# Last layer of a four-layer attention kernel: output product ahead of the pieces, back transposes at the end of a round, pieces and row statistics placed anew

## What is computed

```
ln_out = layernorm(hidden_states, ln1_s, ln1_b)
qkv = ln_out @ w_qkv + b_qkv
ctx = merge_heads(attention(q, k, v, ltor_mask))          # 16 heads of 16
x = hidden_states + ctx @ w_ao + b_ao
q = layernorm(x, ln2_s, ln2_b) @ w_q + b_q;  k, v = split(encoder_states @ w_kv + b_kv)
x = x + merge_heads(attention(q, k, v, cross_mask)) @ w_co + b_co
return x + gelu(layernorm(x, ln3_s, ln3_b) @ w1 + b1) @ w2 + b2
# attention: scores / 4, scores * mask - 10000 * (1 - mask), softmax, @ v
```

## Time and profile before

| | us |
|---|---|
| median of 3 runs | 1341.6 (1341.17 to 1344.08) |
| the profiled execution, its own time | 1344.38 |
| its span in the profile | 1342.6 |
| PE busy | 1249.9 (93% of the span) |
| DVE, ACT, POOL busy | 837.7, 738.5, 568.8 |
| rounds of the last layer | from 1057.58 (first piece of FIRST) to 1342.6 |

### The profile page before, as it was taken

How to read it: one execution, slowest core, us unless ns; L and a number is a source line. 1 busy time by engine, 2 the same in 40 slices (tenths; PEclk the granted TensorE clock), 3 DMA queues, 4 the chain that set the end, 5 groups by cost and what they waited for, 6 DMA issues and landing times.

```text
span 1342.6 us, 24499 instructions
## 1 busy us (share of the span) xinstructions
PE 1249.9 (93%) x8912; PEld 1021.4 (76%) x8912; DVE 837.7 (62%) x1864; ACT 738.5 (55%) x2000; POOL 568.8 (42%) x583
## 2 busy tenths in 40 slices
PE   6999999999887988999999999999998978988788
PEld 5777777777644557899999889999996646767667
DVE  4666666766549976666666776666675137687521
ACT  4665666566546875545454655455544244666621
POOL 3664555555359963232120413131203146677501
PEclk9999999999998999999999999999999989998999
DMA  6101010100010004111111111120001001000000
GB/s 261 50 27 52 27 52 27 53 27 29 3 65 0 1 1 157 33 48 33 48 32 49 33 48 43 37 72 9 17 1 65 0 0 64 2 1 1 1 12 20
DMA packets 15525, 50.44 MB, mean 38 GB/s; under 512 B 1840, under 2 KB 5296, under 8 KB 14384
## 3 DMA queue, kind: packets, MB, share of 16 engines
q1 hardware_dynamic: 15408, 48.87, 11.0%
HBM read 47.82 MB, written 1.05 MB: 36 GB/s over the span
## 4 chain that ended last, share of the span: by engine, by line
PE 81%; DVE 11%; ACT 4%; issue 2%; POOL 1%; DMA 1%; SPq 0%; DVEq 0%; ACTq 0%
PE pS L1534 13%; PE pT L1562 6%; PE acc L1614 6%; PE acc L326 6%; PE pC L406 4%; PE pT L393 4%; PE pS L376 4%; PE pS L1576 4%; PE pC L1599 4%; PE heads_scores L1355 3%; PE acc L362 3%; PE heads_scores L1344 3%; PE pT L1587 2%; PE heads_scores L2041 2%; DVE stats L1248 2%
## 5 line engine op out<-in xcount | busy, mean ns | idle before, releaser
L1534 PE MATMUL pS<-split_sources,split_pair_weights 128*128 128x512 f32 x768 | 212.0, 411 | 5.8 <-issue 4.3
L722 POOL TENSOR_TENSOR probs<-probs,stats 128x512 f32<-128x512 f32 x128 | 130.5, 1040 | 140.1 <-DVE stats L587 140.1
L528 ACT ACTIVATE probs<-pS,stats 128x256 f32<-128x256 f32 x256 | 117.8, 472 | 102.0 <-DVE stats L582 102.0
L1534 PEld LDWEIGHTS pS<-split_sources,split_pair_weights 128*128 128x128 f32 x768 | 135.9, 190 | 30.7 <-issue 6.6
L1711 ACT ACTIVATE probsT<-pT 128x256 f32<-128x256 f32 x128 | 49.1, 384 | 197.2 <-PE pT L1587 197.2
L1614 PE MATMUL acc<-l_wo_parts,l_ctx_parts 128*128 128x256 f32 x768 | 122.0, 295 | 1.0 <-DVE l_ctx_parts L1783 1.0
L1562 PEld LDWEIGHTS pT<-l_wv_parts,split_sources 128*128 128x128 f32 x756 | 106.9, 188 | 14.2 <-issue 2.2
L1562 PE MATMUL pT<-l_wv_parts,split_sources 128*128 128x256 f32 x756 | 110.6, 281 | 2.1 <-issue 2.1
L1837 POOL TENSOR_TENSOR split_pair_weights<-weights_a,split_pair_weights 128x1024 fp32r<-128x1024 f32 x16 | 38.0, 2378 | 170.1 <-ACT split_pair_weights L1675 170.0
L1614 PEld LDWEIGHTS acc<-l_wo_parts,l_ctx_parts 128*128 128x128 f32 x768 | 99.4, 190 | 1.2 <-DVE l_ctx_parts L1783 1.2
L326 PE MATMUL acc<-split_sources,split_pair_weights 128*128 128x512 f32 x372 | 99.5, 402 | 0.8 <-POOL split_pair_weights L704 0.7
(11 more groups left out here) (253 smaller groups left out, 2899.1 us busy)
## 6 DMA issues: line engine op xcount, KB each, us to landing
weights_a<-in_l_w SPq DMA_DIRECT2D x16, 768.5 KB, 4.3
weights_a<-in_l_w SPq DMA_DIRECT2D x16, 768.0 KB, 5.9
value_bias_rows<-in_l_bv SPq DMA_DIRECT2D x16, 256.0 KB, 4.4
weights_b<-in_l_wo SPq DMA_DIRECT2D x16, 256.0 KB, 2.7
w_fc<-in_l_w SPq DMA_DIRECT2D x4, 1024.0 KB, 5.9
bias_rows<-in_rows SPq DMA_DIRECT2D x1, 1536.0 KB, 13.3
x_residual<-in_x_dbl SPq DMA_DIRECT2D x2, 512.0 KB, 7.0
masked_scores<-in_ctx_dbl SPq DMA_DIRECT2D x2, 512.0 KB, 7.9
```

The source lines that it names most:

```text
L528: a = e.activation(self.E[:, n % 4, h, it, :], self.S[h][:, it, :], ACT.Exp, bias=self.st[:, 1, n % 4, h, it:it + 1], accum_out=self.st[:, ...
L722: e.tensor_tensor(self.E[:, n % 4, h, :, :], self.E[:, n % 4, h, :, :], self.st[:, 3, n % 4, h, :].unsqueeze(2).broadcast_to([P, 2, D]), A ...
L1534: mm = e.matmul(bank[:, :], self.w_qk[i % 2][kw][:, 1 - which, c, h * P:h * P + P], g.split[:, which, ks, c, half * HALF:half * HALF + HAL ...
```

## The change

The changed kernel does the same arithmetic with the same instructions, apart from the ACT table loads that follow from the new order (7 of them after the program's first in the changed kernel, 5 before). `attention_output` goes from round t-5 behind the pieces to t-4 ahead of them, with `rows_transposes`, `evacuate_ct` and `add_x` likewise one round earlier; `back_transposes` goes from the start of a round to the end of the round before; on ACT `exps` half 1 and `evacuate_c` go behind `evacuate_t`; on DVE `scale_and_mask` half 1 goes ahead of the maxima; on POOL the shifts go behind `add_masks` of three quarters, `rstd_of` and `add_bias`; the tables FIRST, FILL, STATS and ROWS have new contents.

```diff
--- before.py
+++ after.py
@@ -1931,10 +1931,10 @@
 
     R = 2 * B
     STEPS = R + 10
-    FIRST = ['G0', 'T0', 'G1', 'T1', 'G2', 'K00', 'Q00', 'V00', 'G3', 'K01', 'Q01', 'V01', 'G4']
-    FILL = {0: ['G5'], 1: ['G6', 'G7'], 2: ['U4', 'U5'], 3: ['T2', 'K02', 'Q02', 'U6'], 4: ['U7'], 5: ['T3', 'K03', 'V02', 'Q03'], 6: ['V03', 'J00', 'J01'], 7: ['T4', 'Q10'], 8: ['V10', 'J10'], 9: ['T5', 'Q11'], 10: ['V11', 'J11'], 11: ['T6', 'Q12'], 12: ['V12'], 13: ['T7', 'Q13'], 14: ['V13'], 15: ['T8'], 16: ['H00', 'H01', 'H02', 'H03'], 17: ['T9', 'H10', 'H11'], 18: ['H12', 'H13', 'O0'], 19: ['T10', 'O1', 'O2'], 20: ['H20', 'H21'], 21: ['H22', 'H23'], 22: ['T11', 'O3'], 23: ['H30', 'H31', 'H32', 'H33'], 24: ['O4', 'O5'], 25: ['O6', 'O7']}
-    STATS = {2: [2], 4: [3], 6: [4], 8: [5], 10: [6], 12: [7], 14: [8], 16: [9], 18: [10], 20: [11]}
-    ROWS = {3: [2], 5: [3], 7: [4], 9: [5], 11: [6], 13: [7], 15: [8], 17: [9], 19: [10], 21: [11]}
+    FIRST = ['G0', 'G1', 'T0', 'G2', 'K00', 'T1', 'G3', 'G4', 'Q00', 'Q01', 'G5', 'K01', 'G6', 'G7']
+    FILL = {1: ['U4'], 2: ['V01', 'V00', 'U5'], 3: ['T2', 'U6', 'K02', 'Q02'], 4: ['U7'], 5: ['T3', 'J01', 'K03', 'Q03'], 6: ['J00', 'V02', 'T4'], 7: ['Q10'], 8: ['J11', 'T5', 'V03'], 9: ['V11', 'Q11'], 10: ['J10', 'V10', 'T6'], 11: ['Q12'], 12: ['T7'], 13: ['Q13'], 14: ['V13', 'V12', 'T8'], 15: ['H02'], 16: ['T9', 'H03'], 17: ['H01', 'H12', 'H00', 'H13'], 18: ['T10', 'H11', 'H10', 'H20'], 19: ['O0', 'O1', 'H21'], 20: ['O2', 'T11', 'H23'], 21: ['H30', 'H31'], 22: ['H22', 'H33', 'H32'], 23: ['O3', 'O4'], 25: ['O5', 'O6', 'O7']}
+    STATS = {2: [2], 4: [3], 5: [4], 7: [5], 9: [6], 11: [7], 13: [8], 15: [9], 17: [10], 19: [11]}
+    ROWS = {3: [2], 5: [3], 6: [4], 8: [5], 10: [6], 12: [7], 14: [8], 16: [9], 18: [10], 20: [11]}
 
     def __init__(self, g, cross, m2, weights, masks, w_loaded, masks_ready):
         self.g, self.cross, self.m2 = g, cross, m2
@@ -2177,22 +2177,22 @@
         for sem, value in self.w_loaded[1]:
             wait(e, sem, value)
         for t in range(self.STEPS):
-            if 0 <= t - 4 < self.R:
-                back_transposes(t - 4)
             if 0 <= t - 0 < self.R:
                 scores(t)
             if 0 <= t - 3 < self.R:
                 context(t - 3)
-            if 0 <= t - 5 < self.R:
-                rows_transposes(t - 5)
+            if 0 <= t - 4 < self.R:
+                rows_transposes(t - 4)
             if 0 <= t - 2 < self.R:
                 transposes(t - 2, 0)
+            if 0 <= t - 4 < self.R:
+                attention_output(t - 4)
             for p in self.FILL.get(t, []):
                 self.pe_piece(e, p)
-            if 0 <= t - 5 < self.R:
-                attention_output(t - 5)
             if 0 <= t - 2 < self.R:
                 transposes(t - 2, 1)
+            if 0 <= t - 3 < self.R:
+                back_transposes(t - 3)
 
 
     def act_piece(self, e, p):
@@ -2286,17 +2286,19 @@
         for p in self.FIRST:
             self.act_piece(e, p)
         for t in range(self.STEPS):
-            if 0 <= t - 4 < self.R:
-                evacuate_c(t - 4)
             if 0 <= t - 2 < self.R:
                 exps(t - 2, 0)
+            if 0 <= t - 4 < self.R:
+                evacuate_ct(t - 4)
+            if 0 <= t - 2 < self.R:
+                evacuate_t(t - 2)
             if 0 <= t - 2 < self.R:
                 exps(t - 2, 1)
-            if 0 <= t - 5 < self.R:
-                evacuate_ct(t - 5)
-            if 0 <= t - 2 < self.R:
-                evacuate_t(t - 2)
-            for p in self.FILL.get(t, []):
+            if 0 <= t - 3 < self.R:
+                evacuate_c(t - 3)
+            for p in self.FILL.get(t, [])[:1]:
+                self.act_piece(e, p)
+            for p in self.FILL.get(t, [])[1:]:
                 self.act_piece(e, p)
 
 
@@ -2416,14 +2418,14 @@
                 scale_and_mask(t, 0)
             for q in self.ROWS.get(t, []):
                 self.rows(e, q)
+            if 0 <= t - 0 < self.R:
+                scale_and_mask(t, 1)
             if 0 <= t - 1 < self.R:
                 maxes(t - 1, 0)
+            if 0 <= t - 4 < self.R:
+                add_x(t - 4)
             if 0 <= t - 1 < self.R:
                 maxes(t - 1, 1)
-            if 0 <= t - 0 < self.R:
-                scale_and_mask(t, 1)
-            if 0 <= t - 5 < self.R:
-                add_x(t - 5)
             for p in self.FILL.get(t, []):
                 self.dve_piece(e, p)
             for q in self.STATS.get(t, []):
@@ -2462,22 +2464,22 @@
         for sem, value in self.masks_ready:
             wait(e, sem, value)
         for t in range(self.STEPS):
+            if 0 <= t - 0 < self.R:
+                add_masks(t, 0)
+            if 0 <= t - 0 < self.R:
+                add_masks(t, 1)
+            if 0 <= t - 0 < self.R:
+                add_masks(t, 2)
+            for q in self.STATS.get(t, []):
+                self.rstd_of(e, q)
+            for q in self.ROWS.get(t, []):
+                self.add_bias(e, q)
             if 0 <= t - 1 < self.R:
                 shift(t - 1, 2)
             if 0 <= t - 1 < self.R:
                 shift(t - 1, 3)
             if 0 <= t - 0 < self.R:
-                add_masks(t, 0)
-            if 0 <= t - 0 < self.R:
-                add_masks(t, 1)
-            for q in self.STATS.get(t - 0, []):
-                self.rstd_of(e, q)
-            if 0 <= t - 0 < self.R:
-                add_masks(t, 2)
-            if 0 <= t - 0 < self.R:
                 add_masks(t, 3)
-            for q in self.ROWS.get(t - 1, []):
-                self.add_bias(e, q)
 
 
 def store(g, e, ready, base):
```

## The result

| | before | after |
|---|---|---|
| median of 4 runs, us | 1341.4 | 1310.0 (1308.05 to 1310.21) |
| ratio, 95% interval | | 0.9761 (0.9743 to 0.9779) |
| profiled execution, own time / span | 1344.38 / 1342.6 | 1310.21 / 1308.4 |

The forecast was 1317.6 in a range of 1306 to 1331: right in direction, with the measured time inside the range, and 8 us too cautious. The rival with denser work on PE, 1308.6, lies nearer; the part on the prediction says what of it came true.

What follows compares the result with a forecast made beforehand. A latency loop across engines, none full, was taken as the bound, with some loss to clock. Idle 18.2 plus clock 5.4 gave 23.6, taken as 24 us saved: 1344.4 to 1320.4, less 2.8 for the median, 1317.6; range 1306 to 1331.

Steps and rivals of the forecast that it cites:

- The rival with denser work on PE: Rounds 6 to 25: only two slow places stay, pair of rounds 17.0 us; 33 us saved, 1308.6; chance 0.13.
- What bounded the kernel before: First piece to end: no engine full, latency of a loop bounds it; PE could have worked 43.4 us more.
- The loop of the earlier trace: Output product, `add_x`, statistics, rows, T, `hT`, query piece, next output product: 20.8 us per pair of rounds.
- Rounds 6 to 15: Middle rounds: pair takes 18.0 us, paced by DVE; PE idles 7 us where 17.1 were.
- Rounds 0 to 5: Start: PE waits 7.6 us where 11.4 were, and 1.4 in rounds 4 and 5 where 3.0 were.
- Drain: Rounds 16 on: PE waits 9.2 us where 11.9 were, including `transposes(14, 0)` 1.1 and `transposes(15, 0)` 2.7 late.
- Clock: Slow places behind PE's waits: four or five of eight stay, 7.0 of 12.4 us, so 5.4 saved.
- The sum: Whole changed part: idle 18.2 us and clock 5.4 saved, together 23.6, taken as 24.
- Table loads: ACT in the drain: two more loads at 1.28 us; the Trainium skill's drain would make each 1.4 dearer.
- Rows held by POOL: DVE's two rows take 3.2 us instead of 2.2 beside busier POOL: 14 us saved, 1327.6; chance 0.20.
- ScalarE holding the product: `evacuate_ct` behind `exps` half 0 makes PE stand up to 2.4 us in 16 rounds: 1355.6; chance 0.07.
- Moved waits: Each wait comes back elsewhere, such as POOL's `rstd_of` for statistics; pair stays near 20.8 us: 1341.6; chance 0.04.

Runs made afterwards that it cites:

- U early: The changed kernel with U4, U5, U6 one round earlier, V01 behind T2 in round 3, and H02, H03 in round 18: 1304.7 us, ratio 0.9719.
- H late: The changed kernel with pieces H02 and H03 in round 18 instead of 15 and 16: 1306.5 us, ratio 0.9729.

## Why the prediction was right, point by point

- **What bounded the kernel before**: right. The loop of the earlier trace rows is gone from the chain, and every experiment that undid one part of the change, but for the one on `exps`, cost 9 to 28 us. The places that the prediction named came near too: scores of unit 6 at 1140.61 (1139 forecast) and of unit 15 at 1218.62 (1220).
- **Rounds 6 to 15**: right in kind, too dear in size; this is the mis-sized term. The pair was put at 18.0 us with DVE as the pace setter; it took 17.0 (16.8, 18.7, 16.8, 15.8, 16.9), PE idling 2.6 in place of 7.0. DVE's work is 82.4 / 5 = 16.5, not 17.0: the rows went from 11.2 to 9.5 us, and the stretch holds ten of DVE's copies of transposes where it held eleven. DVE idles 0.5 a pair, not 0.8, because it is often still at work when the transposes land. The rest, 0.2, had been added as caution. That DVE would set the pace is right for rounds 12 to 15 only; in rounds 6 to 11 PE is the full engine, which the 1.4 us of idle time per pair did not foresee.
- **Rounds 0 to 5**: 8.0 and 0.6 idle against 7.6 and 1.4. Scores 1 waited 2.8, U4 1.4, context 0 0.8, T2 1.1.
- **Drain**: 7.9 against 9.2. The context waits are 1.25, 1.08 and 1.08 against 1.1 each; the two waits behind table loads came the other way about, 1.86 and 0.86 for 1.1 and 2.7, because T9's evacuation and a load ran while PE still had work.
- **Clock**: 6.7 us of slow places left against 7.0. The size fits better than the places, which is in part luck: four or five were forecast, at rounds 0 to 1, 13 and 16 to 19, and there are two clusters, none at round 13, 3.7 us at 1084 to 1094 and 3.0 at 1230 to 1237:

```profile
1084.31 2.09 PE L2108 MATMUL heads_scores<-big,qT 32*128 32x256 f32 x16 [2.78 <-DVE masked_scores L2368]
1087.83 6.36 PE L1355 MATMUL heads_scores<-w_fc,hidden_b 128*128 128x256 f32 x16 [1.43 <-DVE probs L2368]
...
1230.58 1.97 PE L2120 MATMUL heads_transposed<-consts,probs 128*128 128x128 f32 x8 [1.86 <-ACT probs L2256]
1232.34 1.92 PE L2159 MATMUL heads_output<-weights_c,value_bias_rows 128*128 128x256 f32 x4
```

- **The sum**: idle 24.3 saved instead of 18.2. PE's busy time fell by 10.2, of which the clock term had 5.4. The slow places of before, added up one by one, come to 13.3 and not 12.4, those of after to 6.7, so the clock gave 6.6. For the other 3.6 there are only rows that fit: a group of matmuls right behind a wait is recorded about 0.1 longer than one that follows another group (query pieces 1.99 in the earlier trace rows, 1.89 after), and one ahead of a wait is counted to its end, while the next group otherwise starts 0.17 before it (transposes at 1155.97 take 1.04, the next group starts at 1156.84). PE has 24 waits after and 42 before; an estimate from these rows, 18 times up to 0.27, is up to 4.9. That was not tested by itself.
- **Table loads**: 1.28 us, and no gap around them beyond waits for PE, at all five loads of the drain, as in the earlier trace rows. The 1380 ns of drain that the Trainium skill (ScalarE: Activation LUTs, What ACT_TABLE_LOAD costs) adds to a switch does not show: the load starts 0.02 after the end of the ACTIVATE before it.
- **Rivals**: the one nearest to the result is the denser PE (1308.6, chance 0.13). Of its two terms the pair of 17.0 us came true to the number, the clock did not: 6.7 us of slow places stayed, not 3.1. Rows held by POOL did not come, they were shorter (0.99 us each on the mean against 1.16), though POOL went from 72% to 94% busy. Within the profile after, the two rows take 1.7 to 2.4 while POOL works and 0.73 at 1253.88 and 1275.08, where it is idle. The Trainium skill (GPSIMD Engine Reference, Specifications) has the two engines share their SBUF interfaces, with contention for VectorE instructions in a 2-port mode or with two SBUF inputs; the trace agrees that they contend, and no row shows in which mode the rows run. ScalarE holding the product is real and small (0.9 us; 4.8 with its order undone). Moved waits: the statistics hold POOL for 44.9 us, less than the 73.9 of before, and in rounds 6 to 15 DVE never waits for POOL.
- **What the prediction missed**: it named POOL's reordering among the edits and gave it no price. Taken out of the new kernel it costs 20 us. The sum takes the rows "at the same point of DVE's round", which holds only if POOL's deviations are ready by then; the text did not say that it rested on POOL's order.

How the parts combine was settled by undoing them. In the old schedule POOL's order alone gives 3, the product alone 6, and all step orders without the tables 4. In the new one, each taken away costs 20, 16 and 28. Before, removing one wait uncovered another (the back transposes' 7.3 us for ACT above, 0.9 before), which fits several waits of similar length beside one path; that reading is argued from the waits and not tested further. After, PE, DVE and POOL are 97%, 97% and 94% busy in the middle rounds, and what is put onto DVE as a wait is paid nearly in full: DVE idles 13.2, 21.2 and 28.2 us more in rounds 6 to 15 with the product behind, POOL's old order and both, and the stretch is 13.0, 20.2 and 29.7 us longer. What the new tables would give with all step orders of before was not tried: the statistics of units 0 and 1 stand in round 5, ahead of the `add_x` that they need in that order.

## What to carry to other kernels

When a software pipeline's chain of waits goes round several engines while none is full, list every step on that loop and move all of them; one move alone may measure as little (3 and 6 us here) and still be needed. Judge a single part by taking it out of the finished version, not by adding it to the old one. On an in-order engine look first for what stands in front of the short producer (here the 0.9 us of deviations behind two shifts and three mask adds): its place cost 20 us.

## What the runs showed of the hardware

- After waits of 2.78 and 1.43 us, with only the scores of unit 1 between them, PE ran at half clock (1.2 GHz): scores 2.09 for 1.15 us and U4 6.36 for 3.62. With 2.32 and 1.44 around scores of 1.15, G6 and G7 took 6.51 for 3.60. Waits of 1.53, 0.64 and 1.43 us around 3.69 us of U4 and the scores, in the version with U early, left PE at full clock.
- The same waits do not always bring the same clock: the product behind waits of 1.08 and 0.47 us takes 1.92 us in the profile of U early and 1.13 in that of H late, and the drain is 1.7 us longer for it. A difference of that size between two single profiles is no effect of an edit by itself.
- The slow place moves with the work: pieces put into the gap of the first scores were themselves run at half clock (6.51 for 3.60), so filling that gap gained nothing that could be measured (1309.7 for 1310.0).
- Two row normalisations of 128x256 on DVE take 0.73 us with POOL idle and 1.66 to 2.38 with POOL at work, in the same kernel; with POOL 94% busy instead of 72% they got no longer (0.99 us each on the mean for 1.16).
